# Packing the third product of the mixer's projections: two heads in one 128-row tile

## The reference

```
# L0_tok: B, F, L, H = (32, 64, 256, 4), D = 64
def proj(w, b):
    y = jnp.einsum('nclh,dc->ndlh', x, w) + b[None, :, None, None]
    return _flatten(y)
q = proj(Wq_w, Wq_b)
k = proj(Wk_w, Wk_b)
v = proj(Wv_w, Wv_b)
ek = jnp.exp(k)
num = jnp.einsum('ts,nsd->ntd', ew, ek * v)
den = jnp.einsum('ts,nsd->ntd', ew, ek)
y = jax.nn.sigmoid(q) * num / den
h = y @ out_w + out_b + _flatten(x)      # then a layernorm
```

## Time and profile before

| | us |
|---|---|
| median of 3 runs | 2207.89 |
| lowest and highest run | 2204.55, 2208.34 |
| the profiled execution, its own time | 2204.59 |
| its span, first to last instruction | 2202.8 |
| TensorE busy (matmuls) | 2081.1 (94%) |
| VectorE busy | 1436.8 (65%) |
| ScalarE busy | 991.9 (45%) |
| GpSimd busy | 684.3 (31%) |

### The profile page before, as it was taken

How to read it: one execution, slowest core, us unless ns; L and a number is a source line. 1 busy time by engine, 2 the same in 40 slices (tenths; PEclk the granted TensorE clock), 3 DMA queues, 4 the chain that set the end, 5 groups by cost and what they waited for, 6 DMA issues and landing times. The chain is left out here.

```text
span 2202.8 us, 42583 instructions
## 1 busy us (share of the span) xinstructions
PE 2081.1 (94%) x15678; PEld 1847.7 (84%) x15678; DVE 1436.8 (65%) x3061; ACT 991.9 (45%) x2044; POOL 684.3 (31%) x737
## 2 busy tenths in 40 slices
PE   5899999999999999999889999999999999999998
PEld 4677777787887877777758999989998888889998
DVE  7677777777777877777644444677754444445666
ACT  2155555455555555554553333322225555554332
POOL 4334334233243343342202111000013333333665
PEclk9999999999999999999999999999999999999999
DMA  2533433424334233344214343000013333334665
GB/s 76 84 66 64 85 62 77 81 54 89 70 65 85 66 73 82 62 80 71 50 39 155 120 135 130 27 23 30 30 44 99 106 104 104 106 103 121 183 182 157
DMA packets 125274, 189.25 MB, mean 86 GB/s; under 512 B 23153, under 2 KB 76418, under 8 KB 125074
## 3 DMA queue, kind: packets, MB, share of 16 engines
q1 hardware_dynamic: 101232, 134.65, 26.0%
q0 software_dynamic: 12736, 34.69, 5.6%
q10 hardware_dynamic: 11106, 17.19, 2.4%
HBM read 84.32 MB, written 49.58 MB: 61 GB/s over the span
## 5 line engine op out<-in xcount | busy, mean ns | idle before, releaser
L675 ACT ACTIVATE pT<-ps 128x514 f32<-128x514 f32 x512 | 304.9, 597 | 308.7 <-PE ps L485 304.0
L842 DVE TENSOR_REDUCE mx<-ps 128x2 f32<-128x512 f32 x512 | 340.7, 680 | 106.1 <-PE ps L468 106.0
L2001 POOL DMA_INDIRECT z<-zd,itab x136 | 128.3, 944 | 470.2 <-DVE itab L1914 253.5
L468 PE MATMUL ps<-km,q 112*128 112x256 f32 x1024 | 246.0, 327 | 16.3 <-DMA km<-klo 10.5
L485 PE MATMUL ps<-q,km 114*128 114x258 f32 x1024 | 228.7, 305 | 31.5 <-ACT pT L675 31.5
L485 PEld LDWEIGHTS ps<-q,km 114*128 114x128 f32 x1024 | 159.1, 189 | 81.0 <-ACT pT L675 54.3
L1291 PE MATMUL ps<-zhi,whi 128*128 128x256 f32 x1056 | 218.4, 289 | 2.5 <-issue 2.4
L468 PEld LDWEIGHTS ps<-km,q 112*128 112x128 f32 x1024 | 166.7, 191 | 58.3 <-issue 24.9
L1291 PE MATMUL ps<-zhi,wlo 128*128 128x256 f32 x1056 | 214.7, 285 | 0.0
L1291 PE MATMUL ps<-zlo,whi 128*128 128x256 f32 x1056 | 213.9, 284 | 0.0
L1319 ACT ACTIVATE sil<-ps 128x512 f32<-128x512 f32 x132 | 79.0, 598 | 264.6 <-PE ps L1291 264.6
(11 more groups left out here) (320 smaller groups left out, 4997.5 us busy)
## 6 DMA issues: line engine op xcount, KB each, us to landing
yd<-raws SPq DMA_DIRECT2D x136, 128.0 KB, 1.8
q<-qhi SPq DMA_DIRECT2D x128, 129.0 KB, 4.1
km<-khi SPq DMA_DIRECT2D x256, 64.5 KB, 3.2
xs<-in_x SPq DMA_DIRECT2D x64, 256.0 KB, 4.4
z<-hscr SPq DMA_DIRECT2D x46, 256.0 KB, 2.9
raws<-in_wu SPq DMA_DIRECT2D x12, 768.0 KB, 4.8
hscr<-h SPq DMA_DIRECT2D x34, 256.0 KB, 5.1
zd<-z SPq DMA_DIRECT2D x33, 256.0 KB, 2.0
```

The source lines that it names most:

```text
L468: last = pe.matmul(ps[:, i % 2, k * L:(k + 1) * L], q2[p % U][0:MAXROW, QAT[g], t * P:(t + 1) * P], km[p % 2][0:MAXROW, k, g, 0:L], start= ...
L675: act.activation(pT[:, 2 * g:2 * g + 2, t, :], ps[:, score_bank(b, n):score_bank(b, n) + 2, 0:N], ACT.Exp, scale=HD ** -0.5).then_inc(s_ok, 1)
L842: dve.tensor_reduce(mx[:, t, 2 * QAT[g]:2 * QAT[g] + 2], ps[:, i % 2, :].rearrange("p (k l) -> p k l", k=2), AX_X, ALU.max, negate=True).t ...
L2001: pool.indirect_dma_start(zg(i), None, zd_rows, bass.IndirectOffsetOnAxis(itab[:, i:i + 1], 0)).then_inc(zg_in[i % NG], 16)
```

## The change

A new tile `xp` holds only rounded x, two heads in its 128 rows: head 2f in rows 0 to 63, head 2f+1 in rows 64 to 127. The third product of two heads is then one matmul. For the queries its weights are wlo twice on the diagonal of a 128x128 block. For keys and values `xp` is held and the weights stream as 256 columns: wlo for the upper rows beside zero, then zero beside wlo for the lower rows, so the sums of the two heads land side by side.

GpSimd writes `xp` in `split_x`, after the cast and before the subtraction (which overwrites rows 64 to 127 of `xh`). There is one `xp`, so the copies of image j wait until the keys and values of image j-1 are done (`kv_ps`); the cast stands ahead of this wait, the subtraction and all else of GpSimd behind it. The weights' tiles change shape, and the filler streams 512 columns of `browr` in place of `wqr`.

```
-    wkvr = sb("wkvr", [P, 2, 2 * C], F32R)
-    wqr = sb("wqr", [P, 2, 2, P], F32R)
+    xp = sb("xp", [P, 2, L], F32R)
+    wkvr = sb("wkvr", [P, 3, 2 * C], F32R)
+    wqr = sb("wqr", [P, 3, P], F32R)
...
-                pe.matmul(ps[:, n, :], wqr[:, 0, 0, :], wqr[:].rearrange("p a b q -> p (a b q)"), start=True, stop=True)
+                pe.matmul(ps[:, n, :], wqr[:, 0, :], browr[:, 0:512], start=True, stop=True)
...
-                for hh in range(2):
-                    for term in range(2):
-                        last = pe.matmul(ps[:, 2, f * L:(f + 1) * L], wqr[:, term, hh, :], xh[p % 2][:, 2 * f + hh, :],
-                                         start=(hh == 0 and term == 0), stop=(hh == 1 and term == 1))
+                for n, x in enumerate((xh[p % 2][:, 2 * f, :], xh[p % 2][:, 2 * f + 1, :], xp[:, f, :])):
+                    last = pe.matmul(ps[:, 2, f * L:(f + 1) * L], wqr[:, n, :], x, start=(n == 0), stop=(n == 2))
...
-                for term in range(2):
-                    last = pe.matmul(ps[:, 3 - t, h * 2 * C:(h + 1) * 2 * C], xh[p % 2][:, h, t * P:(t + 1) * P],
-                                     wkvr[:, term, :], start=False, stop=(h == H - 1 and term == 1),
-                                     skip_group_check=True)
+                pe.matmul(ps[:, 3 - t, h * 2 * C:(h + 1) * 2 * C], xh[p % 2][:, h, t * P:(t + 1) * P],
+                          wkvr[:, 0, :], start=False, stop=False, skip_group_check=True)
+            for f in range(FT):
+                last = pe.matmul(ps[:, 3 - t, f * 4 * C:(f + 1) * 4 * C], xp[:, f, t * P:(t + 1) * P],
+                                 wkvr[:, 1:3, :].rearrange("p n w -> p (n w)"), start=False, stop=(f == FT - 1),
+                                 skip_group_check=True)
...
-        dve.tensor_tensor(wkvr[:, 1, :], wkv[:, 1, :], wkvr[:, 1, :], ALU.subtract)
-        dve.tensor_tensor(wqr[:, 1, :, :], wq[:, 1, :, :], wqr[:, 1, :, :], ALU.subtract)
+        dve.tensor_tensor(wkvr[:, 1:3, :], wkv[:, 1:3, :], wkvr[:, 1:3, :], ALU.subtract)
+        dve.tensor_tensor(wqr[:, 2, :], wq[:, 2, :], wqr[:, 2, :], ALU.subtract)
...
-            pool.wait_ge(xround_ok, j + 1)
+            pool.wait_ge(xround_ok, 2 * j + 1)
+            if later(j):
+                pool.wait_ge(kv_ps, 2 * j)
+            pool.tensor_copy(xp[C:P, :, :], xh[p % 2][C:P, 1:H:2, :]).then_inc(xround_ok, 1)
+            pool.tensor_copy(xp[0:C, :, :], xh[p % 2][0:C, 0:H:2, :])
+            pool.wait_ge(xround_ok, 2 * j + 2)
```

More of the change, by code:

```diff
@@ L91, in stage_a @@
     bdm = temp(FT, P)
-    wkv, wq, idn = temp(2, 2 * C), temp(2, 2, P), temp(C)
+    wkv, wq, idn = temp(3, 2 * C), temp(3, P), temp(C)
     brow = temp(H * 2 * C + D)
@@ L2049, in layout @@
     tiles = lambda m: f(m.reshape(-1, P, m.shape[1]).transpose(1, 0, 2))
-    wkv, wq = z(P, 2, 2 * C), z(P, 2, 2, P)
+    wkv, wq = z(P, 3, 2 * C), z(P, 3, P)
     both = np.concatenate([t["tok_Wk_w"].T, t["tok_Wv_w"].T], axis=1)
[L2052 to L2056, removed]
+    for k in range(2):
+        rows = slice(k * C, (k + 1) * C)
+        wkv[rows, 0] = both
+        wkv[rows, 1 + k] = both
+        for hh in range(2):
+            wq[rows, hh, hh * C:(hh + 1) * C] = t["tok_Wq_w"].T
+        wq[rows, 2, k * C:(k + 1) * C] = t["tok_Wq_w"].T
     o["wkv"], o["wq"] = wkv, wq
```

## The result

| | median of 5 runs | lowest to highest | profiled execution | its span |
|---|---|---|---|---|
| before | 2208.34 us | 2204.55 to 2209.77 | 2204.6 us | 2202.8 us |
| after | 2190.26 us | 2188.93 to 2195.27 | 2191.04 us | 2189.2 us |

The ratio is 0.9923, 95% interval 0.9907 to 0.9938: the change makes the kernel 0.8% faster, 18.1 us by the medians where 8.1 were forecast. Between the two profiled executions the gain is 13.6 us; the other 4.5 come from where those two lie among their own repeats (the profiled execution of before was 3.7 us under its median, that of after 0.8 over). One execution of all that follow, of z_early_before, took 3384.3 us at a mean granted clock of 0.56 and is left out of every figure.

The account below looks back on a forecast made before the run. TensorE was taken to bound the steady steps: -10.4 (keys and values), -0.6 (image 2) and +2.9 (start) sum to -8.1 us, from median 2207.9 to 2199.8. Range 2196 to 2204; with rivals 1 to 3, 2190 to 2206.

Parts of the forecast that it names:

- Queries, 0 a step: `mixer_q` in a steady step: two fewer matmuls spare 0.24 us, all taken up by TensorE's wait for `z`; value 0.
- Rival 1: Queries: their 0.24 us a step counts too, if `z` comes earlier with them; 7.0 us more, 2192.8; chance 0.08.
- Keys and values, 0.36 a step: `mixer_kv`: 9 matmuls become 7, 0.18 us saved per tile, 0.36 per image, 10.4 over 29 steps.
- Nothing waits behind them: Behind keys and values: `clso` falls to 0.16 us, maxima come some 2 us earlier, so the whole 0.36 is kept.
- GpSimd's block under cover: Steady step: GpSimd's copies and moved subtraction end about 627.5, before VectorE's L793 at 633.00; cost 0.
- rival 4: Steady step: GpSimd's moved block reaches L793, if the pair costs 7 us; each us beyond costs 29; chance 0.05.
- The start, +2.9: First images, GpSimd's copies uncovered: +2.0 at the first subtraction, +1.6 in image 1's split, -0.7 in image 2's.
- Rival 2: GpSimd's two copies run side by side: pair 1.0 us, start cost 0, time 2196.9; chance 0.14.
- Rival 3: Keys' DMA binds: the 11 steps waiting on it don't get shorter, 4.0 us lost, 2203.8; chance 0.13.

Follow-up runs that it names:

- z_early_before: Kernel before with ScalarE writing `z` earlier (values' copy one slot earlier, class row's exponentials behind the gate): 2199.97 us, ratio 0.9981.
- q_only: Changed kernel with only the queries using the pair tile, keys and values as before: 2204.61 us, ratio 1.0000 to the kernel before.
- cast_first: Changed kernel with ScalarE writing `z` earlier and GpSimd's class-row subtraction `pcl` behind the cast: 2175.80 us, ratio 0.9866 to the kernel before.
- cast_first_q8: Same as cast_first, but only keys and values use the pair tile, queries keep their 8 matmuls: 2183.52 us, ratio 0.9907 to the kernel before.
- kv_no_third: Changed kernel with the keys' and values' third product left out, 5 matmuls a tile instead of 7: 2174.34 us in one run.
- kv_only: Changed kernel with only keys and values using the pair tile, queries keeping 8 matmuls: 2197.70 us, ratio 0.9960 to the kernel before.
- two_xp: Changed kernel with two pair tiles in turn, so GpSimd's copies and subtraction need not wait for keys and values: 2194.03 us, ratio 0.9932 to before.
- z_early_after: Changed kernel with ScalarE writing `z` earlier, by the same reordering as z_early_before: 2193.84 us, ratio 0.9931 to the kernel before.
- after_again: Changed kernel unchanged, timed again beside the kernel before: 2192.47 us, ratio 0.9930.

## Why the prediction was right, and where its sizes were off

The account holds in its mechanism; the time fell inside the wider range partly by luck. None of the rivals that widened it held as written, and of the 10.0 us between the forecast's gain and the measured one, 8.0 (3.5 behind the last `mixer_out`, 4.5 between traces and medians) are scatter that the change has no known part in.

**Queries, 0 a step: right.** The wait for `z` grew from 0.31 to 0.55, as written. q_only has an unchanged step, and cast_first against cast_first_q8 gives the 0.24 back once that wait is gone. Rival 1 falls.

**Keys and values, 0.36 a step: right in kind, 0.43 measured.** The term that was mis-sized is the saving per tile, 0.18, which stopped at the tile's end. From the first 128-column matmul to the maxima (L468, now L469) it went nearly as forecast: 0.68 us (612.98 to 613.66) against 0.84 in the earlier trace rows, and 0.66 had been written. But the pair of maxima matmuls behind it now takes 0.24 (613.66 to 613.90), where before it took 0.29, from the 619.51 of the earlier trace rows to the scores (L485):

```profile
619.80 0.41 PE L485 MATMUL ps<-q,km 114*128 114x258 f32 x2
```

The weight loads (start, us, engine, operation) show where it comes from, before and then after:

```profile
618.44 1.09 PEld L379 LDWEIGHTS ps<-wkvr,xh 128*128 128x128 f32 x8
619.45 0.30 PEld L468 LDWEIGHTS ps<-km,q 112*128 112x128 f32 x2
```

```profile
612.74 0.65 PEld L377 LDWEIGHTS ps<-wkvr,xh 128*128 128x128 f32 x4
...
613.54 0.31 PEld L469 LDWEIGHTS ps<-km,q 112*128 112x128 f32 x2
```

Before, the eight loads took 1.01 us from start to the next group's (618.44 to 619.45) and the eight matmuls 0.84: the loads had used up their lead, and the first load of the next group began only 0.06 before its matmul, against 0.12 now (613.54 to 613.66). That the next group pays for this is argued from the rows, but kv_no_third bears it out: there the pair stands right behind four short matmuls, with a load 0.06 ahead (604.26 and 604.32), and takes 0.30 (to 604.62). Over the whole stretch, tile and pair together, it is 1.13 against 0.92, 0.21 a tile. The same as a difference: eight short matmuls take 0.84 us and four take 0.39 (612.98 to 613.37), so the second four cost 0.45 and not the 0.42 of the mean; less 0.24 for the two of 256 columns, that is 0.21. Over 28 steps the 0.43 in place of 0.36 make 2.0 us more than forecast. The Trainium skill, TensorE: Matmul & The Clock Gate, section Back-to-back issue gap, gives a sustained 81 ns at 128 columns, from which the prediction estimated a saving of 0.08 a tile. The trace does not agree: eight took 0.105 us each, and the measured 0.21 a tile lies farther from 0.08 than the forecast's 0.18 did.

**Nothing waits behind them: right.** kv_only and after keep 0.42 and 0.43. The further claim, that a blocked `clso` would leave only 0.2 of 0.36, was not tried as it stands, since two_xp missed the block. z_early_after shows the mechanism with the cast in the subtraction's place: 0.28 us of wait in 27 steps. That is more than the 0.16 claimed, in a step that is shorter by 0.24 in front.

**GpSimd's block under cover: right.** GpSimd ended at 621.10, which is 26.6 us into the step, and L1104 behind it waited 8.42 us for its input. L794, the danger of rival 4, kept its 0.7.

**The start, +2.9: wrong. Up to image 3's `mixer_out` it was +0.1, where 2.9 - 0.6 - 0.36 = +1.9 was forecast.** Three terms failed. The pair costs 1.33 us (9.97 to 11.30), not 2.05: the two copies read and write rows without the stride of four words that the cast has, and the cast's rate was the wrong row to take (that the stride makes the difference is argued, since the two also differ in size). VectorE also got in between the operations of GpSimd at one more place than I had put it: its first cast (10.66) took 0.80 us and only the second (11.38) was held, 3.00. Behind the first split VectorE was 0.87 us late and not 2.0. In image 1's split two of its operations and not one got in beside the pair (22.46 and 23.21), and otherwise VectorE is held twice there in either kernel, for 2.71 and 3.03 us before and 2.48 and 2.95 after; that place added 0.16 and not 1.6. So the first sum of the mixer came 1.03 us later, and not 3.6. In image 2's split L794 was not held at all, since it fell at 62.10, just between the two copies, and the second copy stretched to 1.10. It took 0.69 us where L793 had taken 2.63, and ended at 62.79 against 63.23, although the split's cast began 1.68 us later than in before (59.41 and 57.73). This place gave back 2.0 us, from 1.57 late to 0.43 early, and not 0.7. Then the keys' DMA took 3.94 us of TensorE's time at 71.52 (0.33 before), and by 95.61 against 95.60 the two kernels were level.

**Rival 2, copies side by side: falls.** The second starts 0.67 after the first, which takes 0.61. The time at the start that this rival gave came nearly true, by another cause. The Trainium skill, GPSIMD Engine Reference, section Instruction dispatch, says that each core goes on when its own rows are done. The trace does not agree for this pair: two copies on disjoint halves of the rows started 0.67 us or more apart in all 32 splits.

**Rival 3, the keys' DMA binds: a small part of it is true.** after has ten such waits with 7.2 us, before eleven with 6.4, and the 28 steps kept 10.2 of 12.0 us. That is 1.8 us and not 4.0, in the steps with such a wait; the waits themselves make some 1.2 of it (between these two `mixer_out` ten in either kernel, 5.93 us before and 7.15 after).

**The rest.** The forecast and the traces differ by 5.5 us (8.1 and 13.6): 1.8 up to image 3's `mixer_out`, 3.5 behind the last, and 0.1 in the 28 steps, where 2.0 more by the tile (28 x 0.07) and 1.8 less by the DMA cancel. The further 4.5 us between traces and medians are scatter: in after_again's rounds the medians lie 14.6 us apart (2207.11 and 2192.47), not 18.1.

## What to carry to other kernels

Price the work that you take off an engine from the first instruction of the group to a point where the engine's rows look the same with and without it, not to the next instruction: here the tile gave 0.16 and the pair behind it another 0.05. And price it as the difference of two lengths rather than by the mean: here the last four of eight matmuls cost more than the first four. When a saving goes into a wait, the wait is worth an experiment of its own. Here ScalarE's order gave nothing alone in the changed kernel (33.09 for 33.10), since a 128x4 copy of VectorE then ran into GpSimd's cast, and with GpSimd's order put right too the two moves gave 0.54 us a step, more than the change itself. When GpSimd work is moved, look at each VectorE operation that works from SBUF to SBUF and at which GpSimd operation runs as it comes due and which follows, and not only at sums of busy time.

## What the runs showed of the hardware

- A GpSimd copy of 64x512 without a stride takes 0.61 us, and 0.67 from start to start, where the cast of 128x1024 through a stride takes 2.04: 1.2 ns an element of a row against 2.0. No run separates stride and size.
- A VectorE copy within SBUF that comes due while GpSimd works is held at least until the current GpSimd operation ends. It may then get in ahead of the next one: `clso` in two_xp (0.57), L945 at the start (0.80), whereas L946 right behind it was held for the whole subtraction (3.00). Or it may not: in z_early_after and z_early_before `clso` came due under `pcl` and was held through the cast behind it as well (2.57, 2.67). So being held can cost the rest of one GpSimd operation and the whole of the next, and what decides between the two stays open.
- The reverse exists too: the second copy at 62.17 took 1.10 us and not 0.61, beside L794 on VectorE from 62.10 to 62.79.
- Two executions of one kernel can differ by 12 us in 200 us in which TensorE has no gap, at a mean granted clock of 0.98 in one and 0.91 in the other: 1694 and 1592 matmuls from 1200 to 1400 us.
- Eight fp32r matmuls of 128 columns, each with a weight load of its own, take 0.84 us and four take 0.39: the second four cost 0.45.
